# Last six slots in an order of their own on every engine, and output weights freed head by head, in an FP32 attention kernel

## The reference

```python
x = x + tanh(g_xattn[0]) * autocorrelation(layernorm(x), ctx, ctx)
x = x + tanh(g_ffn[0])   * routed_ffn(layernorm(x))
# third: 32 query heads of 128 in 8 groups, one key and value head for each group
q = rmsnorm((layernorm(x) @ Wq.T) per head, q_norm_w)
k = rmsnorm((ctx @ Wk.T) per head, k_norm_w); v = (ctx @ Wv.T) per head
probs = softmax(q @ k.T / sqrt(128) + mask)
x = x + tanh(g_xattn[1]) * ((probs @ v) @ Wo.T)
# fourth: a dense layer and the sum of 8 low-rank layers
n = layernorm(x)
x = x + tanh(g_ffn[1]) * (n @ W.T + bias + sum_e((n @ A_e.T) @ (2 * w_e * B_e.T)))
```

## Time and profile before

| | |
|---|---|
| median of 3 runs | 743.99 us (740.37 to 744.77) |
| the profiled execution's own time | 738.72 us |
| its span in the trace | 736.9 us |
| PE busy | 712.1 us, 97% |
| DVE busy | 566.4 us, 77% |
| ACT, POOL busy | 377.6 us, 51%; 371.8 us, 50% |
| DMA | 110.31 MB, 150 GB/s on the mean |

### The profile page before, as it was taken

One profiled execution on the slowest core, in us unless ns is written; L12 is line 12 of the kernel. 1 busy time (PEld: TensorE's weight loads), 2 busy tenths in 40 slices (PEclk: granted clock), 3 DMA queues, 4 the chain that ended last, 5 costly groups with the idle time before them and its releaser, 6 DMA issues.

```text
span 736.9 us, 12666 instructions
## 1 busy us (share of the span) xinstructions
PE 712.1 (97%) x3684; PEld 573.4 (78%) x3684; DVE 566.4 (77%) x1171; ACT 377.6 (51%) x1094; POOL 371.8 (50%) x429
## 2 busy tenths in 40 slices
PE   8899999988999999999999999999999999998996
PEld 5455556577888888888888888888888888887774
DVE  4888887566788777777877787787778787778784
ACT  5567664355555545544564545465545654454220
POOL 2568866556444634553564346345625642265331
PEclk9999999999999999999999999999999999999999
DMA  8400104145765675666657665756665666446221
GB/s 307 144 29 30 43 16 158 42 132 147 228 172 156 180 218 141 180 194 182 167 162 215 161 174 143 235 148 186 194 179 149 167 188 200 119 124 161 67 90 63
DMA packets 109283, 110.31 MB, mean 150 GB/s; under 512 B 12576, under 2 KB 78240, under 8 KB 108960
## 3 DMA queue, kind: packets, MB, share of 16 engines
q1 hardware_dynamic: 109216, 109.51, 52.6%
HBM read 69.62 MB, written 39.85 MB: 149 GB/s over the span
## 4 chain that ended last, share of the span: by engine, by line
PE 30%; POOL 21%; issue 16%; DMA 13%; DVE 11%; ACT 5%; SPq 4%; DVEq 0%; ACTq 0%; POOLq 0%
DMA pTf<-p_scratch 7%; POOL qkr L617 6%; POOL wo_lo L604 6%; PE pair L959 5%; PE pair L961 5%; PE pair L960 5%; DMA p_scratch<-p_blocks 4%; DVE qkn L1434 4%; SPq L458 3%; PE pair L999 3%; POOL wq_lo L596 2%; POOL prob L609 2%; PE pair L973 2%; POOL wkv_lo L586 2%; DVE p_blocks L1409 1%
## 5 line engine op out<-in xcount | busy, mean ns | idle before, releaser
L805 ACT ACTIVATE prob<-score,nmax 128x128 f32<-128x128 f32 x256 | 99.8, 391 | 147.8 <-DVE nmax L1399 147.8
L609 POOL TENSOR_TENSOR prob<-prob,erec 128x512 f32<-128x512 f32 x64 | 66.7, 1042 | 123.0 <-DVE erec L1419 123.0
L959 PE MATMUL pair<-wo_hi,oT_hi 128*128 128x512 f32 x256 | 107.3, 419 | 1.2 <-POOL wo_lo L604 1.2
L959 PE MATMUL pair<-wq_hi,nT_hi 128*128 128x512 f32 x256 | 101.7, 397 | 1.3 <-DVE qkn L1434 1.3
L960 PE MATMUL pair<-wo_lo,oT_hi 128*128 128x512 f32 x256 | 100.1, 391 | 0.0
L960 PE MATMUL pair<-wq_lo,nT_hi 128*128 128x512 f32 x256 | 100.0, 391 | 0.0
L961 PE MATMUL pair<-wo_hi,oT_lo 128*128 128x512 f32 x256 | 100.0, 391 | 0.0
L961 PE MATMUL pair<-wq_hi,nT_lo 128*128 128x512 f32 x256 | 100.0, 390 | 0.0
L1424 DVE TENSOR_REDUCE qkss<-qksq 128x5 f32<-128x640 f32 x64 | 52.4, 819 | 48.5 <-ACT qksq L812 48.2
L617 POOL TENSOR_TENSOR qkr<-qkse,neghalf 128x5 f32<-128x5 f32 x64 | 76.7, 1198 | 5.3
L812 ACT ACTIVATE qksq<-pair 128x640 f32<-128x640 f32 x64 | 45.0, 703 | 65.7 <-PE pair L961 65.7
(11 more groups left out here) (171 smaller groups left out, 1700.8 us busy)
## 6 DMA issues: line engine op xcount, KB each, us to landing
qk_scratch<-qk_blocks SPq DMA_DIRECT2D x256, 80.0 KB, 1.9
qkT<-qk_scratch SPq DMA_DIRECT2D x64, 320.0 KB, 3.0
p_scratch<-p_blocks SPq DMA_DIRECT2D x256, 64.0 KB, 1.8
pTf<-p_scratch SPq DMA_DIRECT2D x64, 256.0 KB, 3.4
wq_raw<-in_wq SPq DMA_DIRECT2D x32, 256.0 KB, 4.1
wo_raw<-in_wo SPq DMA_DIRECT2D x32, 256.0 KB, 4.8
wkv_raw<-in_wkv SPq DMA_DIRECT2D x8, 512.0 KB, 4.9
ctxn<-in_ctx_n SPq DMA_DIRECT2D x8, 256.0 KB, 3.3
```

The costliest lines, as they stand in the source:

```text
L609: pool.tensor_tensor(prob[:], prob[:], erec[:].unsqueeze(2).broadcast_to([P, BL, P]), ALU.mult).then_inc(normed, 1)
L805: t = act.activation(prob[:, i, :], score[:, i, :], ACT.Exp, bias=nmax[:, i:i + 1], accum_out=esum[:, i:i + 1])
L959: pe.matmul(out, l_hi, r_hi, start=start, stop=False)
```

## The change

Four edits in the code:

1. For slots 61 to 66 (N - 3 to N + 2) each of PE, DVE, ACT and POOL runs a function `last_slot(n)` in place of `slot(n)`, with the steps of each slot written out. Slots 67 to 70 are gone, and their steps stand in slot 66. The steps are the same ones, and each has the semaphores that it had.
2. On SP, in slot 62, the read of `qkT` for step 63 stands ahead of the write of the probabilities of step 61.
3. `project_out(8g-1)` counts a new semaphore, `wo_free`, up after each of its first three heads. `high_wo` of the first three heads waits for that in place of the whole product. Head 0 moves to slot 8g + 2, on ACT ahead of `exponents` and on POOL behind `inverse_norms`. Heads 1 to 3 stay in slot 8g + 3.
4. `feed_forward` can be cut in two: for batch 4 two chunks come before `project_out(63)` and two behind it.

The core of the diff (on PE, ACT and POOL the old rows of the last stage in `slot` are taken out, as shown for PE; DVE's `last_slot` is shown for the slots that matter most):

```diff
 # SyncE
-                    if n < 2 and on(n + 1):
+                    if on(n + 1) and (n < 2 or n == N - 2):
                         read_qk(n + 1)
                     if on(n - 1):
                         write_probs(n - 1)
-                    if n >= 2 and on(n + 1):
+                    if on(n + 1) and 2 <= n < N - 2:
                         read_qk(n + 1)
 # POOL
                     if on(n) and n > B and n % B == WO_AT:
-                        for h in range(HG):
+                        for h in range(1, HG):
                             low_wo(g, h)
                     if on(n + 2):
                         inverse_norms(n + 2)
+                    if on(n) and n > B and n % B == WO_AT - 1:
+                        low_wo(g, 0)
...
+                def last_slot(n):
+                    if n == N - 3:
+                        norm_probs(n - 1)
+                        d_scale(1)
+                        inverse_norms(n + 2)
+                        low_weights(CH - 1)
+                    elif n == N - 2:
+                        norm_probs(n - 1)
+                        d_scale(2)
+                        last_bias(0)
+                        norm_probs(n)
+                    elif n == N - 1:
+                        d_scale(3)
+                        last_bias(1)
+                        norm_probs(n)
+                    elif n < N + 2:
+                        d_scale(n - N + 4)
+                        last_bias(n - N + 2)
+                    else:
+                        d_scale(6)
+                        last_bias(4)
+                        last_bias(5)
+                        last_bias(6)
+                        d_scale(7)
+                        last_bias(7)
 # ACT
-                    need(act, y_done, B * g)
+                    if h < HG - 1:
+                        need(act, wo_free, (HG - 1) * (g - 1) + h + 1)
+                    else:
+                        need(act, y_done, B * g)
...
+                    if on(n) and n > B and b == WO_AT - 1:
+                        high_wo(g, 0)
                     if on(n):
                         exponents(n)
...
+                def last_slot(n):
+                    if n == N - 3:
+                        high_out(n - 3)
+                        scale_keys(n)
+                        high_probs(n - 2)
+                        high_v(n + 1)
+                        high_weights(CH - 1)
+                        squares(n + 2)
+                        high_batch(0)
+                        scale_keys(n + 1)
+                        exponents(n)
+                    elif n == N - 2:
+                        high_out(n - 3)
+                        high_batch(1)
+                        high_probs(n - 2)
+                        high_v(n + 1)
+                        exponents(n)
+                        scale_keys(n + 1)
+                    elif n == N - 1:
+                        high_out(n - 3)
+                        high_batch(2)
+                        high_probs(n - 2)
+                        exponents(n)
+                    elif n == N:
+                        high_out(n - 3)
+                        high_batch(3)
+                        high_probs(n - 2)
...
 # PE
-                    if batch(n, FEED) is not None:
-                        feed_forward(batch(n, FEED))
-                    if batch(n, TURN) is not None:
-                        turn_batch(batch(n, TURN))
                     if on(n):
                         scores(n)
...
+                def last_slot(n):
+                    if n == N - 3:
+                        probs_v(n - 3)
+                        project_qkv(n + 2)
+                        turn_batch(0)
+                        scores(n)
+                        project_out(n - 3)
+                    elif n == N - 2:
+                        probs_v(n - 3)
+                        turn_batch(1)
+                        scores(n)
+                        feed_forward(0)
+                        project_out(n - 3)
+                    elif n == N - 1:
+                        probs_v(n - 3)
+                        turn_batch(2)
+                        feed_forward(1)
+                        scores(n)
+                        project_out(n - 3)
+                    elif n < N + 2:
+                        probs_v(n - 3)
+                        turn_batch(n - N + 3)
+                        feed_forward(n - N + 2)
+                        project_out(n - 3)
+                    else:
+                        probs_v(N - 1)
+                        turn_batch(5)
+                        feed_forward(4, (0, 1))
+                        project_out(N - 1)
+                        feed_forward(4, (2, 3))
+                        turn_batch(6)
+                        feed_forward(5)
+                        turn_batch(7)
+                        feed_forward(6)
+                        feed_forward(7)
 # DVE
+                def last_slot(n):
+                    if n == N - 3:
...
+                        low_probs(n - 2)
+                        norm_batch(1)
+                        sum_squares(n + 2)
...
+                        low_batch(0)
+                        mask_and_max(n)
+                        scale_qk(n + 2)
+                        turn_qk(n + 2)
+                    elif n == N - 2:
+                        add_out(n - 4)
+                        low_out(n - 3)
+                        reciprocals(n - 1)
+                        low_batch(1)
+                        low_v(n + 1)
+                        low_probs(n - 2)
+                        turn_probs(n - 1)
+                        mask_and_max(n)
+                        norm_batch(2)
+                        reciprocals(n)
+                        add_out(n - 3)
+                        turn_probs(n)
+                    elif n == N - 1:
+                        low_out(n - 3)
+                        low_batch(2)
+                        low_probs(n - 2)
+                        add_batch(0)
+                        norm_batch(3)
+                        mask_and_max(n)
+                    elif n == N:
+                        add_out(n - 4)
+                        reciprocals(n - 1)
+                        low_out(n - 3)
+                        low_batch(3)
+                        turn_probs(n - 1)
+                        low_probs(n - 2)
+                        add_batch(1)
+                        norm_batch(4)
+                    elif n == N + 1:
+                        add_out(n - 4)
+                        low_out(n - 3)
+                        low_batch(4)
+                        low_probs(n - 2)
+                        add_batch(2)
+                        norm_batch(5)
+                    else:
+                        add_out(n - 4)
+                        low_out(n - 3)
+                        low_batch(5)
+                        add_batch(3)
+                        norm_batch(6)
+                        add_out(N - 1)
+                        add_batch(4)
+                        low_batch(6)
+                        norm_batch(7)
...
```

109 lines of the change are left out of this document (64 added, 45 removed).

## The result

The changed kernel takes **724.61 us**, the median of four runs (723.9 to 725.99), where the kernel before takes 743.98 beside it (740.37 to 744.77, four runs): ratio 0.9751, 95% interval 0.9716 to 0.9786. The forecast was 730.8, and its range began at 725.0, so the result lies 0.4 us outside it. For the profiled execution it was 725.5 us, and that one took 725.99, so the two profiled executions lie 12.7 us apart and the medians 19.4. Most of what follows is about these two numbers.

The account below looks back on a forecast made before the run. PE's own work bounds the steady slots, so only its waits at the weights and in the last 60 us could go: 3.6 + 9.6 = 13.2 us off the median 743.99 gives 730.8 us, range 725 to 738.

Parts of the forecast that it names:

- Weights, 3.6 us: Slots where output weights change: PE's 0.53 us wait for `wo_lo`, seven times, goes; gain 3.6 us, between 0 and 3.7.
- the walk: The prediction's slot-by-slot timing of the new order, for the moved weights and the last slots; no wait over 0.5 us.
- The end, 9.6 us: Last 60 us: 11.5 us lost to PE's five waits, restarts and low clock, less 1.9 left over; gain 9.6 us.
- The longest wait: PE's 3.23 us ahead of `feed_forward(0)`, behind step 62's key copy; goes with restart and low clock, 5.1 us.
- The low clock: Behind PE's 3.23 us wait: 3.4 of 10 us at 1.2 GHz, costing 1.7 us, which goes.
- (a): `project_out(60)`: `low_out` stands behind `turn_probs(62)` on DVE; PE waits 0.1 us.
- (b): `project_out(61)`: the mask of step 63 stands behind five DVE instructions; PE waits 0.5 us.
- (c): `low_probs(62)` beside POOL's bias addition makes `norm_batch(4)` late; `turn_batch(4)` waits 0.4 us.
- (d): Last probabilities' DMA holds DVE: copy at 704.6; `turn_batch(5)` waits 0.4 us and `project_out(63)` 0.4 us.
- (e): Behind the last `project_out`: products cover the last batch's norm, turn and split; waits of 1.75 and 1.46 us go.
- DVE as the bound: Rival, slots 62 to 66: DVE's queue 1 us later, five PE waits each grow 1 us; 735.8 us, chance 0.20.
- The slower case: Rival, slots 62 to 66: late exponents hold DVE, PE waits 3.2 us and its clock falls repeatedly; 754 us, chance 0.04.

Follow-up runs that it names:

- experiment 7: Same run as `end_only`: the kernel before with the steps of slots 66 to 70 in the changed kernel's order; 738.09 us, ratio 0.9972.
- Experiments 5 and 6: Kernel before with `high_batch(0)` and `scores(62)` moved ahead: 741.36 us; that plus step 63's key read earlier and key copy behind the exponents: 738.08 us.
- (9): Changed kernel with the read of step 63's keys on SP put back behind the probabilities' write; 724.97 us, ratio 0.9767 to the kernel before.
- Experiment 12: Changed kernel with one unused `bn_stats` more on DVE at the start of each of slots 62 to 65; 725.94 us.
- `turn_first`: Kernel before with `high_batch(0)` ahead of step 62's key copy on ACT and `scores(62)` ahead of `feed_forward(0)` on PE; 741.36 us, ratio 1.0014.
- Experiment 10: Changed kernel with POOL's bias additions of batches 2 and 3 moved to slot 63 and of batch 4 to slot 65; 725.3 us, ratio 0.9776.
- `after_again`: The changed kernel measured once more, no edit; 724.82 us beside 741.93 for the kernel before, ratio 0.9771.
- `same`: The kernel before measured once more, no edit; 741.72 us beside 740.03, ratio 1.002.
- `wo_freed`: Kernel before with the head-by-head semaphore `wo_free` alone, all four heads staying in slot 8g+3; 739.73 us, ratio 0.9997.
- `wo_only`: Kernel before with the output weights' edit (edit 3) alone; 736.92 us, ratio 0.9954.
- `end_only`: Kernel before up to slot 65, then the steps of slots 66 to 70 in the changed kernel's order; 738.09 us, ratio 0.9972.

## Why the prediction was right, and where not

**The bound and the places.** Right. A plain slot is 8.47 us in both kernels, and all of the gain in the trace lies in the slots of the weights and in the last 60 us.

**Weights, 3.6 us.** S4 to S61 was shortened by 2.84 us in the profiled pair. One late read in slot 42 took 0.8 of it. Over all traces, the mean of the seven with the weights moved is 486.97 us and that of the seven without 490.81, so 3.8 us; that is above the 3.7 of all seven waits, and single slots (5, 6, 11, 43) differ from trace to trace by more than that. Behind the scores' start, the steps of the walk came within 0.25 us on ACT and 0.2 on POOL. The spare "1 us" is less when DMA delays POOL: it was gone in slot 43.

**The end, 9.6 us.** 59.29 - 48.83 = 10.46 us. The longest wait with what hung on it: S61 to S63 fell by 6.55 us, where the sum has 3.23 + 1.62 + 2 x 0.16 + 1.7 = 6.87. Most of the 0.3 us between them is the wait of 0.2 us at `scores(62)`, where the walk had none. The low clock was sized right for this trace: granted clocks of 0.91, 0.50 and 0.73 in the slices 680 to 682, 682 to 684 and 684 to 686 make 1.7 us. What was left over behind S63 was put at 1.9 us and was 0.7: (a) was 0.20 us for 0.1, (b) 0.21 for 0.5, (c) 0.29 at `turn_batch(4)` for 0.4, and of (d), 0.8 us, nothing came. The way round of the last probabilities was right to 0.1 us: the copy stands at 702.30, where the walk, less the 2.3 us by which the end begins earlier in this trace, has 704.6 - 2.3. But PE began `probs_v(63)` at 704.85 and not at 704.4, and `norm_batch(5)`, done at 704.78, was ahead of `turn_batch(5)` at 705.54. (e) is right, and experiment 7 gives it by itself: 3.49 us.

**The two turned steps and the read on SP.** The prediction spoke of both as if the turn took the wait away, with the earlier read to keep it away. Experiments 5 and 6 show that the turn alone is worth 0, and with the earlier read and the copy of step 63 behind the exponents 3.9 us. In the changed kernel the earlier read is worth nothing (9). What the prediction walked through without naming it as a cause is the order of exponents and key copy of step 63 in slot 62. With that order the read may come late. Whether the earlier read would have done without that order was not run, so the share of each in the 3.9 us stays open.

**The rivals.** DVE as the bound was given 0.20 and a delay of five times 1 us. Experiment 12 added some 2.6 us to its queue and cost 1.1 us at most. It did not hold the queue back by 1 us at five places, so the price as such was not tested: where DVE was 0.75 us later, at `project_out(60)`, PE waited 0.6 us more, and the loss was made good behind it. The slower case did not come in the changed kernel, but its mechanism is what `turn_first` shows in one slot: a wait of 4.92 us, and the lower clock (0.51 from 690 to 694 us).

**The rule on shared access.** The Trainium skill (SBUF — State Buffer, Who interferes with whom) has DVE with two SBUF inputs and GpSimd in an instruction that reads SBUF exclude each other. Experiment 10 agrees, 1.64 us against 0.65. Of the two more pairs that the prediction named, `low_probs(60)` took 0.97 us for 0.67 and `norm_batch(6)` 0.77 for 0.54, well under the 1 us allowed for, and one that it did not name, `low_probs(61)` beside `last_bias(1)`, took 1.08. The first two put no wait on PE behind them in the rows, so the sum stood.

**The number.** The step that failed is "I take the same 13.2 us off the median". It treats before's distance from its profiled execution, 5.3 us, as something that the change leaves as it is. The runs show that part of it was the old order's own. S61 to S63 is 22.9 us in the mean of the five traces in which those slots are unchanged (21.75 to 24.62), and 15.4 in the new order (15.29 to 15.55): 7.5 us, 1.0 more than in the profiled pair. With 3.8 for the weights and 3.9 for S63 to the last matmul (37.31 to 33.40), the traces give 15.2 us. The medians side by side give 14.8 (`ff_whole`, which lacks edit 4), 17.1 and 19.4, because before has medians of 743.98, 741.93, 740.03 and 739.58 in four sessions, the first of them from four runs only, and the changed kernel 724.61 and 724.82. The three later sessions were on three chips, so that the chip may have a part in it. What before loses on top in its longer executions was not traced. Those over 743 us have a mean clock of 0.991 to 0.993, where the traced ones have 0.995. Beside `after_again`, 743.9 us goes with 0.991 and 739.14 with 0.995, and 0.004 of 740 us is 3 of these 4.8 us, as an estimate. That fits more time at the lower level, but no trace shows where. So it stays open what made up the last 4 of the 19.4 us, and that the median of four runs came out so far from the profiled execution was in part luck.

## What to carry to other kernels

Where a profile shows one wait behind an in-order engine, look for what will be at the head of the queue when it is gone: undoing one inversion moved 3.23 us to a place where it cost more, and the gain came only with the second inversion undone and the turns moved ahead too. A full queue is the bound only where its results meet their demand; count the cover in front of each result and not the idle time. And if the waits that a change removes hang on transfers, part of the spread goes with them: subtract from the profiled execution, or trace before several times, before subtracting from a median.

## What the runs showed of the hardware that was not expected

Four writes to DRAM of 64 KB each, in one group, held SP's queue for 1.76 us in slot 62 of two traces and for 2.6 to 3.2 us in four others, where the program around them is the same or nearly so.

The clock fell in or right behind waits of 3.23 us (before), 3.15 (`same`), 3.35 (`wo_freed`), 3.26 (`wo_only`), 4.51 (`end_only`) and 4.92 (`turn_first`). What the lower level took there (in each slice of the trace, its length by one less the granted clock) was 1.7 us in four of the six and 3.4 us in `wo_freed` and `turn_first`; in `turn_first` some 1.3 of it fell while PE still waited, by the same rows. But in `end_only` it is 1.00 behind the wait of 3.18 us, as long as the one of before:

```profile
680.00:690.00 10.00, 7.02 (x37) 6.00 (x38) 7.68 (x14) 3.27 (x13) 4.59 (x5) 1.00 0.30 72
690.00:700.00 10.00, 5.49 (x21) 4.17 (x20) 5.06 (x8) 3.42 (x12) 3.10 (x4) 0.83 0.29 76
```

```profile
682.98 0.47 PE L990 MATMUL pair<-cT_hi,nT_hi 128*128 128x512 f32 x1 [3.18 <-DVE nT_lo L1499]
```

Ahead of the scores of step 3 it is the same. Ten traces have a wait of 2.89 to 2.94 us there. Behind it the clock is 0.50 to 0.52 from 176 to 178 us in eight of them, and in `wo_freed` and `ff_whole` it stays at 1.00. The row of that slice in the changed kernel and in `ff_whole`:

```profile
176.00:178.00 2.00, 2.00 (x6) 0.50 0.00 0
176.00:178.00 2.00, 2.00 (x9) 1.00 0.00 0
```

In the other four traces that wait was 1.3 to 1.4 us, and the clock did not fall behind it. So at this length the same wait may or may not cost the clock, and the term of 1.7 us in the prediction was a draw as well.
